# Gated slot attention kernel: queries held one place later than in time, and a new order at the end of each slot

## The chip, the cores and the metric

The kernel runs on one core of a Trainium2 chip. The metric is the device time of one execution in microseconds (us), and the kernel's time is the median of several executions. TensorE is called PE, its weight loads PEld, VectorE DVE, ScalarE ACT, GpSimd POOL, and SyncE, which issues most of the DMAs, SP.

## The reference

An attention layer with a gated two-state recurrence (B=4 sequences, T=512, 256 channels, H=16 heads of 128), a layer norm, a gated feed-forward layer with int8 weights, and a second layer norm. All is fp32. The core of it:

```python
def step(carry, xs):                       # per head, over time
    Sk, Sv = carry
    q_t, k_t, v_t, w_t, g_t, b_t = xs
    gt = jnp.exp(g_t)
    bw = b_t[:, :, None] * w_t
    Sk = Sk * gt[:, :, None, :] + k_t[..., :, None] * bw[:, :, None, :]
    Sv = Sv * gt[..., None] + bw[..., None] * v_t[:, :, None, :]
    s = jnp.einsum('bhd,bhdm->bhm', q_t, Sk) * SCALE
    a = jax.nn.softmax(s, axis=-1)
    o_t = jnp.einsum('bhm,bhmd->bhd', a, Sv)
    return ((Sk, Sv), o_t)
...
q = short_conv(h @ Wq, cq); k = short_conv(h @ Wk, ck)      # 4 taps, then silu
v = short_conv(h @ Wv, cv); w = short_conv(h @ Ww, cv)
g = jax.nn.log_sigmoid(h @ Wf1 @ Wf2)
beta = jax.nn.sigmoid(h @ Wb)
w = l2norm(rs(w, M))
...
o = gsa2_scan(q, k, v, w, g, beta)
o = o * rsqrt(mean(o * o) + EPS) * norm_w * sigmoid(h @ Wg1 @ Wg2 + bg2)
return o @ Wo
...
x = layernorm(x + attn(x));  x = layernorm(x + ffn(x))
```

## The kernel before, in words

A unit is one head of one sequence, so there are 64. The program runs in 68 slots. In each slot four units are in flight at different stages: `u1` (projections, convolutions, gates), `u2` (keys against queries, first scan), `u3` (softmax, second scan, output), `u4` (norm, gate, output projection), and `u5`, whose result is added to a sum in DRAM. Every engine has its own program, written out by hand: the order of the calls in the slot's loop over `r` (0 to 8) is the order on the engine, and engines meet by semaphores only. Buffers are few, and PSUM is fully used: `proj_ps` (2 banks), `tr_ps`, `V_ps`, `mix_ps` (2), `work_ps` (2).

A recurrence with decay is done without a loop over time, by blocks that double: 9 levels, of which levels 0 to 6 lie inside chunks of 128 places. At a level the queries of one block see the keys of the block before it. `U` holds the keys' weights as seen from the end of their block; they are grown on DVE level by level: `copy_U` copies the blocks that this level needs, `scale_U` multiplies the even blocks by the gates' products, in two instructions. For `u1` the levels 0 to 3 are grown at the end of a slot, for the same unit as `u2` levels 4 to 7 at the start of the next one.

The first scan (`level_scores` on PE, `descend` on DVE) goes from the largest block down and leaves the scores in `V_ps`: ACT copies them to `V`, PE turns them (`turn(1, V)`), DVE takes the rows' largest (`largest`, tile `mx`), ACT takes the exponentials (`exp_scores`, tile `aN`), PE turns `aN`, ACT copies that to `W`. The second scan goes up: `mix_products` on PE (W against U), `mix` on DVE (into `A2`, by masks), `grow_W` on POOL. `outputs` on PE adds the products of `A2` with the values and of `W` with the chunk states `Sv`.

A query at place t sees the keys up to and with t. In blocks this means that a block's queries are those from its predecessor's last place to its own last but one: the views are shifted by L - 1 places (`after_odd`). The last place of each chunk falls out of the second scan's views, so it has four products of one column (`mix_ends`), a copy of four columns (`mixable`, lev 0) and a growth of its own (`grow_W_ends`).

At the end of a slot ACT's order is: `oN` (copy of the attention output), `V`, then `tanh(act, u1, 2)`, which is the tanh of k and an instruction that adds 1; POOL multiplies k's two parts by that (`silu_qk`, i = 2, tile `qk`), and PE's `key_query` of the next slot waits for it. Every fourth slot a new head follows (`next_h`): there POOL also splits weights into two parts (`low_weights`, L370, and `low_f`, L387), and DVE takes `largest` of `u2` in the slot itself rather than at the start of the next.

At the end of the attention the feed-forward layer runs in 32 steps, and SP stores one sequence after another to `out`.

## Time and profile before

| | |
|---|---|
| median of 3 runs | 2008.67 us (2008.37 to 2124.88) |
| profiled execution | 2009.03 us |
| its span | 2007.3 us |
| PE busy | 1927.6 us (96%) |
| DVE busy | 1775.8 us (88%) |
| ACT busy | 1396.5 us (70%) |
| POOL busy | 1334.0 us (66%) |
| granted TensorE clock, mean | 0.984 |

Busy time is the sum of the times in which an engine has an instruction in it; instructions of one engine overlap by some tens of ns at their ends. The span is that of the profiled execution, from first to last instruction; 1.7 us of the execution lie outside it.

### The profile page before, as it was taken

The numbers are of one execution on the slowest core, as the hardware profiler recorded it, in microseconds if no ns is written. First come the engines' busy times: TensorE is split into PE (matmuls) and PEld (weight loads), VectorE is DVE, ScalarE is ACT, GpSimd is POOL, SyncE is SP. The second block draws the span as 40 slices with busy tenths as digits, with TensorE's granted clock in tenths as the row PEclk, the third lists the DMA queues.
The fourth block names the chain that finished last, engine by engine and source line by source line (L and its number), as shares of the span: only waits on it lengthen the run. The fifth ranks groups of instructions, "written<-read, shape, count | busy, mean of one in ns | idle before, by whom it ended". The sixth has DMA issues, their size and how long they took to land.

```text
span 2007.3 us, 41500 instructions
## 1 busy us (share of the span) xinstructions
PE 1927.6 (96%) x12192; PEld 1627.1 (81%) x12192; DVE 1775.8 (88%) x4096; ACT 1396.5 (70%) x3986; POOL 1334.0 (66%) x2289
## 2 busy tenths in 40 slices
PE   7899999999999999999999999999999999999697
PEld 5688888888888888888888888888888888887586
DVE  5599999999999999999999999999999999998487
ACT  4477777777777777777777777777777777776442
POOL 5367676767677676777677776777676766766343
PEclk8899999999999999999999999999999999999798
DMA  3011110111111111111111111111110111102300
GB/s 78 1 55 26 25 35 14 36 24 33 26 24 26 26 34 23 27 24 32 26 27 23 27 34 24 26 24 33 26 34 15 29 32 23 22 15 51 63 11 32
DMA packets 53645, 58.51 MB, mean 29 GB/s; under 512 B 14896, under 2 KB 44720, under 8 KB 53424
## 3 DMA queue, kind: packets, MB, share of 16 engines
q0 software_dynamic: 9216, 33.56, 11.4%
q1 hardware_dynamic: 44208, 22.29, 4.0%
q8 instruction: 104, 1.70, 0.4%
q14 instruction: 117, 0.96, 0.2%
HBM read 20.19 MB, written 37.75 MB: 29 GB/s over the span
## 4 chain that ended last, share of the span: by engine, by line
PE 82%; POOL 8%; DVE 5%; issue 3%; ACT 1%; DMA 1%; POOLq 0%; DVEq 0%; ACTq 0%
PE proj_ps L718 15%; PE mix_ps L802 11%; PE V_ps L773 10%; PE work_ps L927 8%; PE work_ps L933 7%; PE tr_ps L742 6%; PE V_ps L751 5%; PE work_ps L1569 5%; PE proj_ps L397 4%; PE work_ps L822 3%; PE mix_ps L809 2%; POOL w_lo L370 2%; PE tr_ps L782 2%; PE work_ps L824 2%; POOL qk L618 1%
## 5 line engine op out<-in xcount | busy, mean ns | idle before, releaser
L587 DVE SCALAR_TENSOR_TENSOR conv<-proj_ps,coefs,conv 128x511 f32<-128x511 f32 (+2 forms) x768 | 561.9, 732 | 9.5 <-ACT conv L347 2.6
L298 POOL TENSOR_TENSOR W<-W,tot 128x256 f32<-128x256 f32 x384 | 256.0, 667 | 244.0 <-PE mix_ps L802 243.9
L1053 POOL TENSOR_TENSOR A_lev<-A,masks 128x256 f32<-128x256 f32 x448 | 319.5, 718 | 0.1
L802 PE MATMUL mix_ps<-W,U 128*128 128x128 f32 x1792 | 295.3, 287 | 13.7 <-POOL W L298 8.2
L802 PEld LDWEIGHTS mix_ps<-W,U 128*128 128x128 f32 x1792 | 256.5, 192 | 40.2 <-issue 24.5
L773 PE MATMUL V_ps<-A_lev,UT 128*128 128x128 f32 x1792 | 285.9, 282 | 1.6 <-DVE V_ps L683 1.6
L711 DVE COPY_PREDICATED A<-masks,mix_ps 128x256 f32<-128x256 uint32 x448 | 268.7, 600 | 12.3 <-PE mix_ps L802 12.2
L580 DVE TENSOR_TENSOR wT<-wT,tot 128x128 f32<-128x128 f32 x768 | 233.3, 344 | 40.3 <-DVE U L563 1.8
L773 PEld LDWEIGHTS V_ps<-A_lev,UT 128*128 128x128 f32 x1792 | 237.4, 192 | 23.4 <-DVE V_ps L683 23.2
L356 ACT ACTIVATE th<-conv 128x512 f32<-128x512 f32 x256 | 162.3, 634 | 104.2 <-DVE conv L587 103.0
L718 PE MATMUL proj_ps<-hT_hi,w_hi 128*128 128x512 f32 x512 | 222.9, 435 | 4.5 <-DVE conv L587 2.7
L563 DVE COPY U<-wT 128x256 f32<-128x256 f32 x448 | 206.4, 461 | 7.2
L429 ACT ACTIVATE UT<-tr_ps 128x512 f32<-128x512 f32 (+1 forms) x256 | 139.1, 543 | 103.2 <-PE tr_ps L742 102.4
L683 DVE TENSOR_TENSOR V_ps<-V_ps,tot 128x256 f32<-128x256 f32 x384 | 164.1, 427 | 50.3 <-PE V_ps L773 50.0
L718 PE MATMUL proj_ps<-hT_hi,w_lo 128*128 128x512 f32 x512 | 203.2, 397 | 0.0
L718 PE MATMUL proj_ps<-hT_lo,w_hi 128*128 128x512 f32 x512 | 202.1, 395 | 0.0
L927 PE MATMUL work_ps<-qk 128*128 128x512 f32 (+3 forms) x512 | 182.1, 457 | 3.9 <-POOL qk L618 2.9
L298 POOL TENSOR_TENSOR W<-W,gT 128x256 f32<-128x256 f32 x64 | 54.3, 849 | 197.4 <-PE mix_ps L802 197.4
L347 ACT ACTIVATE conv<-proj_ps,coefs 128x512 f32<-128x512 f32 x256 | 175.6, 686 | 9.2 <-PE proj_ps L718 9.2
L414 ACT ACTIVATE A<-work_ps,fac 128x512 f32<-128x512 f32 (+3 forms) x256 | 128.2, 530 | 63.4 <-PE work_ps L927 63.1
L656 ACT ACTIVATE y_sb<-work_ps,rms 128x256 f32<-128x256 f32 x256 | 107.4, 472 | 63.0 <-PE work_ps L1569 58.8
L742 PE MATMUL tr_ps<-ident,U 128*128 128x128 f32 x896 | 140.1, 273 | 0.0
(200 smaller groups left out, 4774.0 us busy)
## 6 DMA issues: line engine op xcount, KB each, us to landing
head_sum<-y_sb POOLq DMA_DIRECT2D x64, 512.0 KB, 6.5
w_raw<-in_L_attn_Ww SPq DMA_DIRECT2D x16, 128.0 KB, 2.2
w_raw<-in_L_attn_Wq SPq DMA_DIRECT2D x16, 128.0 KB, 2.2
w_raw<-in_L_attn_Wk SPq DMA_DIRECT2D x16, 128.0 KB, 2.3
w_raw<-in_L_attn_Wv SPq DMA_DIRECT2D x16, 128.0 KB, 2.2
wo_raw<-in_L_attn_Wo SPq DMA_DIRECT2D x16, 128.0 KB, 2.0
head_sum<-in_L_attn_hidden_states SPq DMA_DIRECT2D x1, 2048.0 KB, 10.3
acc<-head_sum SPq DMA_DIRECT2D x4, 512.0 KB, 3.9
```

Source lines behind the costliest of these rows:

```text
L298: nc.gpsimd.tensor_tensor(w, w, block_tot(u3.par, lev, 0), ALU.mult).then_inc(W_step, 1)
L347: nc.scalar.activation(conv[:, CONV_BUF[i], :], proj_ps[:, CONV_BANK[i], :], ACT.Copy, scale=filt(u, i, KW - 1)).then_inc(tap_done, 1)
L563: nc.vector.tensor_copy(Ulev(u, lev).rearrange("p (n e l) -> p n e l", e=2, l=L), merged(X, lev))\
L580: nc.vector.tensor_tensor(x_, x_, odd_tot(u.par, lev, e), ALU.mult).then_inc(U_step, 1)
L587: nc.vector.scalar_tensor_tensor(y_, proj_ps[:, CONV_BANK[i], 0:T - back], filt(u, i, KW - 1 - back), y_, ALU.mult, ALU.add).then_inc(conv ...
L711: nc.vector.copy_predicated(dst, mask_cols(lev).bitcast(U32), mix_cols(lev % 2, lev)).then_inc(mix_done, 1)
L718: last = nc.tensor.matmul(dst, w[:, k, :], x_(k), start=(k == 0 and n == 0), stop=(k == KT - 1 and n == 2))
L742: last = nc.tensor.transpose(tr_ps[:, n * P:(n + 1) * P], block_, ident[:, :])
L773: last = nc.tensor.matmul(dst, UT[:, i % 2, at:at + P], A_lev[:, lev, 2 * p:2 * p + 2, :], start=False, stop=True, skip_group_check=True)
L802: last = nc.tensor.matmul(mix_ps[:, half, p * P:(p + 1) * P], Ulev(u3, lev)[:, p * P:(p + 1) * P], after_odd(W[:, p * T // 2:(p + 1) * T / ...
L927: nc.tensor.matmul(work_ps[:, A_BANK[c], c * P:T], qk[:, 1, c * P:(c + 1) * P], qk[:, 0, c * P:T], start=True, stop=True).then_inc(A_ps_re ...
L1053: nc.gpsimd.tensor_tensor(dst, diag_after_odd(lev), mask_cols(lev), ALU.mult)\
```

## The change

Queries are held one place later than in time: place t holds the query of time t - 1, and place 0 that of time T - 1. The first scan is as it was; the shift is made where `V_ps` is copied to `V`. In the second scan the blocks' queries are then simply the odd blocks (`odd` in place of `after_odd`), and no chunk's last place falls out: `mix_ends`, its copy on DVE and `grow_W_ends` on POOL are gone. The query of time T - 1 sees all keys, so there is a fourth chunk state (one more product in `chunk_states`, one more instruction in `states`) and one more product in `outputs`. The gate, the running sum in DRAM and the stores to `out` are shifted in the same way. `vT` has no buffer of its own any more.

Apart from this, ACT's order at a slot's end is changed, and DVE's `copy_U` of level 4 goes from the start of a slot to the end of the one before.

```diff
-            w = after_odd(W[:, :], lev)
+            w = odd(W[:, :], lev)
...
-        def grow_W_ends(pool, u3):
-
-            pool.wait_ge(ends_ready, u3.count(1, 1))
-            ends = W[:, :].rearrange("p (c t) -> p c t", t=P)[:, :, P - 1]
-            nc.gpsimd.tensor_tensor(ends, ends, tot[:, u3.par, T - 8:T - 4], ALU.mult).then_inc(W_step, 1)
...
             dve.wait_ge(tanh_done, u.count(4, 4))
             wait(dve, vT_ps_ready, u.count(1, 0))
+            wait(dve, aT_ps_ready, u.count(1, 0))
...
-            if lev == 0:
-                dve.wait_ge(ends_ready, u3.count(1, 1))
-                nc.vector.tensor_copy(A2[:, :, P - 1], mix_ps[:, 0, T // 2:T // 2 + C]).then_inc(far_done, 1)
...
-            dst = after_odd(A2[:, :, :].rearrange("p c t -> p (c t)"), lev).rearrange("p (c n) l -> p c n l", c=C)
+            dst = odd(A2[:, :, :].rearrange("p c t -> p (c t)"), lev).rearrange("p (c n) l -> p c n l", c=C)
...
-            for c, at in ((0, 2), (1, 1), (2, 3)):
+            for c, at in ((0, 2), (1, 1), (2, 3), (3, 4)):
                 last = nc.tensor.matmul(tr_ps[:, c * P:(c + 1) * P], UT_top[:, at, :], vN[:, u2.par % 2, c * P:(c + 1) * P],
                                         start=True, stop=True)
...
-        def mix_ends(pe, u3):
-
-            for c in range(C):
-                last = nc.tensor.matmul(mix_ps[:, 0, T // 2 + c:T // 2 + c + 1], chunk_of(U_chunks(u3), c),
-                                        W[:, (c + 1) * P - 1:(c + 1) * P], start=True, stop=True)
-            last.then_inc(ends_ready, 1)
...
                 if t:
                     last = nc.tensor.matmul(dst, W[:, cols], Sv[:, u3.par % 2, t - 1, :], start=False, stop=True)
+                else:
+                    last = nc.tensor.matmul(dst[0:1, :], W[:, 0:1], Sv[:, u3.par % 2, C - 1, :], start=False, stop=True,
+                                            skip_group_check=True)
...
-                nc.sync.dma_start(out_v[:, b * C:(b + 1) * C, :], acc[:, b * C:(b + 1) * C, :]).then_inc(ffn["store"], 16)
-            sp.wait_ge(ffn["store"], 16 * B)
+                nc.sync.dma_start(out[b, P - 1:T - 1, :].rearrange("(c p) n -> p c n", p=P), acc[:, b * C + 1:(b + 1) * C, :])\
+                    .then_inc(ffn["store"], 16)
+                nc.sync.dma_start(out[b, 0:P - 1, :], acc[1:P, b * C, :]).then_inc(ffn["store"], 16)
+                nc.sync.dma_start(out[b, T - 1:T, :], acc[0:1, b * C, :]).then_inc(ffn["store"], 16)
+            sp.wait_ge(ffn["store"], 16 * 3 * B)
...
                 for lev in range(GROWN_EARLY, LEVELS - 1):
-                    if u2:
+                    if u2 and lev == GROWN_EARLY:
+                        scale_U(dve, u2, lev)
+                    elif u2:
                         grow_U(dve, u2, lev)
```

The running sum's start value, one DMA of 2048 KB before, is now copied by six DMAs, one of them of 508 rows. The two low and high parts of the gate's input are made in three instructions instead of two, four times in all.

On DVE, around the end of a slot in which no new head follows; `Sv` are the chunk states, the `U` copies and the pairs of `wT` behind them the levels 2, 3 and so on, `mx` is `largest`. Before:

```order
L587 SCALAR_TENSOR_TENSOR conv<-proj_ps,coefs,conv 128x509
L695 SCALAR_TENSOR_TENSOR Sv<-Sv,tot,tr_ps 128x128 x2
L563 COPY U<-wT 128x256
L580 TENSOR_TENSOR wT<-wT,tot 128x32x4 x2
L563 COPY U<-wT 128x256
L580 TENSOR_TENSOR wT<-wT,tot 128x16x8 x2
L540 TENSOR_REDUCE mx<-work_ps 128x4
L563 COPY U<-wT 128x256
L580 TENSOR_TENSOR wT<-wT,tot 128x8x16 x2
```

Now:

```order
L585 SCALAR_TENSOR_TENSOR conv<-proj_ps,coefs,conv 128x509
L694 SCALAR_TENSOR_TENSOR Sv<-Sv,tot,tr_ps 128x128 x3
L561 COPY U<-wT 128x256
L578 TENSOR_TENSOR wT<-wT,tot 128x32x4 x2
L561 COPY U<-wT 128x256
L578 TENSOR_TENSOR wT<-wT,tot 128x16x8 x2
L561 COPY U<-wT 128x256
L538 TENSOR_REDUCE mx<-work_ps 128x4
L578 TENSOR_TENSOR wT<-wT,tot 128x8x16 x2
```

There is a third state, and the copy of level 4 now stands ahead of `mx`.

On ACT at the same place; `oN` is the attention output, `V` the scores, `th` k's tanh and then that plus 1, `tg` the gate of `u4`, `aN` the exponentials. Before:

```order
L1253 ACTIVATE Sv<-tr_ps 128x128
L1257 ACTIVATE oN<-work_ps 128x512
L1262 ACTIVATE V<-V_ps 128x512
L356 ACTIVATE th<-conv 128x512
L360 ACTIVATE th<-th 128x512
L1134 ACTIVATE tg<-proj_ps,bg_sb 128x512
```

Now:

```order
L1254 ACTIVATE Sv<-tr_ps 128x128
L354 ACTIVATE th<-conv 128x512
L358 ACTIVATE th<-th 128x512
L1261 ACTIVATE V<-V_ps 128x511
L1262 ACTIVATE V<-V_ps 128x1
L1266 ACTIVATE oN<-work_ps 128x512
L1135 ACTIVATE tg<-proj_ps,bg_sb 128x512
```

The two instructions on k went ahead of `V`, `V` became two instructions, and `oN` went behind it.

## Rows read from the trace of the kernel before

**Rows 1.** The page, the chain that ended last, share of each engine.

```profile
PE 82%; POOL 8%; DVE 5%; issue 3%; ACT 1%; DMA 1%; POOLq 0%; DVEq 0%; ACTq 0%
```

**Rows 2.** Chain in order of time, one slot: start us, us, what.

```profile
1012.83 0.68 PE work_ps L822 x4
1013.52 0.22 PE work_ps L824 x2
...
1015.81 0.66 PE work_ps L933 x4
1016.47 2.85 PE proj_ps L718 x12
1019.31 0.44 PE work_ps L933 x4
...
1022.72 0.79 PE mix_ps L809 x8
...
1047.94 1.56 PE work_ps L927 x4
```

**Rows 3.** Timeline of DVE: start us, us, engine, line, op [idle before it].

```profile
1013.52 0.78 DVE L695 SCALAR_TENSOR_TENSOR Sv<-Sv,tot,tr_ps 128x128 f32<-128x128 f32 x2
...
1015.54 0.49 DVE L580 TENSOR_TENSOR wT<-wT,tot 128x128 f32<-128x128 f32 x2
1016.50 0.69 DVE L540 TENSOR_REDUCE mx<-work_ps 128x4 f32<-128x512 f32 x1 [0.47 <-PE work_ps L933]
1017.11 0.79 DVE L563 COPY U<-wT 128x256 f32<-128x256 f32 x1
1018.01 0.84 DVE L580 TENSOR_TENSOR wT<-wT,tot 128x128 f32<-128x128 f32 x2
1018.89 0.29 DVE L563 COPY U<-wT 128x256 f32<-128x256 f32 x1
...
1025.53 0.36 DVE L677 TENSOR_SCALAR V_ps<-V_ps,tot 128x129 f32<-128x129 f32 x1
```

**Rows 4.** Timeline of POOL in the same stretch.

```profile
1014.52 1.37 POOL L637 TENSOR_TENSOR tot<-tot 128x32 f32<-128x32 f32 x4
1017.01 1.49 POOL L618 TENSOR_TENSOR qk<-th,conv 128x256 f32<-128x256 f32 x2 [1.12 <-ACT th L360]
```

**Rows 5.** Timeline of ACT in the same stretch.

```profile
1015.16 0.59 ACT L1262 ACTIVATE V<-V_ps 128x512 f32<-128x512 f32 x1
1015.64 0.63 ACT L356 ACTIVATE th<-conv 128x512 f32<-128x512 f32 x1
...
1017.41 0.36 ACT L404 ACTIVATE aN<-work_ps,mx 128x128 f32<-128x128 f32 x1
...
1018.69 0.22 ACT L404 ACTIVATION_READ_ACCUMULATOR aN<-work_ps,mx 128x1 f32 x1
```

**Rows 6.** Timelines of DVE and POOL where a new head follows.

```profile
1042.63 1.10 DVE L580 TENSOR_TENSOR wT<-wT,tot 128x128 f32<-128x128 f32 x2
...
1044.53 0.69 DVE L540 TENSOR_REDUCE mx<-work_ps 128x4 f32<-128x512 f32 x1
...
1043.55 1.52 POOL L370 TENSOR_TENSOR w_lo<-w_raw,w_hi 128x256 fp32r<-128x256 f32 x2
...
1046.37 1.52 POOL L618 TENSOR_TENSOR qk<-th,conv 128x256 f32<-128x256 f32 x2
```

**Rows 7.** Groups of instructions: count, busy us, mean ns, idle before.

```profile
L809 PE MATMUL mix_ps<-W,wT 128*128 128x1 f32 x512 | 61.6, 241 | 0.0
L706 DVE COPY A<-mix_ps 128x4 f32<-128x4 f32 x64 | 9.9, 155 | 6.3 <-PE mix_ps L809 6.3
L1241 ACT ACTIVATE bg_sb<-bg_sb 128x16 f32<-128x16 f32 x1 | 0.2, 226 | 0.0
```

**Rows 8.** Waits: who for whom, us in total, times, longest.

```profile
POOL qk L618 <- ACT th L360: 63.0, 49, 6.5
```

**Rows 9.** The page's DMA issues: count, KB each, us to landing.

```profile
out_x<-acc SPq DMA_DIRECT2D x4, 512.0 KB, 3.1
```

More of the change, by code:

```diff
@@ L214, in pairs, with odd @@
             return ap.rearrange("p (n e l) -> p n e l", e=2, l=1 << lev)
+        def odd(ap, lev):
+            return pairs(ap, lev)[:, :, 1, :]
         def after_odd(ap, lev):
@@ L593, in silu_w @@
             dve.wait_ge(tanh_done, u.count(4, 1))
-            wait(dve, ends_ready, u.count(1, 1 - 2))
+            wait(dve, UT_ps_ready, u.count(6, 2 - 12))
             wait(dve, mix_ps_ready, u.count(7, 1 - 14))
@@ L622, in gates @@
             act.wait_ge(fexp_done, u1.count(1, 1))
-            wait(act, W_step, u1.count(8, 1 - 16))
+            wait(act, W_step, u1.count(7, 1 - 14))
             wait(act, V_step, u1.count(10, -10))
@@ L630, in gate_products @@
                 pool.wait_ge(gate_set, u1.count(1, 1))
-                wait(pool, Sv_step, u1.count(2, 2 - 8))
+                wait(pool, Sv_step, u1.count(3, 3 - 12))
             else:
@@ L670, in descend @@
             if r == 0:
-                wait(dve, V_done, u2.count(1, 0))
+                wait(dve, V_done, u2.count(2, 0))
                 nc.vector.memset(V_ps[:, 0:P], 0.0).then_inc(V_step, 1)
@@ L733, in turn_U @@
             if i == 0:
-                wait(pe, Sv_step, u2.count(2, 0))
+                wait(pe, Sv_step, u2.count(3, 0))
                 pe.wait_ge(U_step, u2.count(22, 22))
@@ L869, in first_copies @@
         def first_copies(act, b):
-            for i, dst in enumerate((f1_hi, g1_hi)):
-                act.wait_ge(first_ps, 2 * b + i + 1)
-                nc.scalar.activation(dst[:, b * T:(b + 1) * T], mix_ps[:, i, :], ACT.Copy).then_inc(first_sb, 1)
-        def first_lows(dve, b):
-            cols = slice(b * T, (b + 1) * T)
-            for i, (dst, high_) in enumerate(((f1_lo, f1_hi), (g1_lo, g1_hi))):
-                dve.wait_ge(first_sb, 2 * b + i + 1)
-                nc.vector.tensor_tensor(dst[:, cols], mix_ps[:, i, :], high_[:, cols].bitcast(F32), ALU.subtract)\
-                    .then_inc(first_lo, 1)
+            act.wait_ge(first_ps, 2 * b + 1)
+            nc.scalar.activation(f1_hi[:, b * T:(b + 1) * T], mix_ps[:, 0, :], ACT.Copy).then_inc(first_sb, 1)
+            act.wait_ge(first_ps, 2 * b + 2)
+            nc.scalar.activation(g1_hi[:, b * T + 1:(b + 1) * T], mix_ps[:, 1, 0:T - 1], ACT.Copy).then_inc(first_sb, 1)
+            nc.scalar.activation(g1_hi[:, b * T:b * T + 1], mix_ps[:, 1, T - 1:T], ACT.Copy).then_inc(first_sb, 1)
+        def first_lows(dve, b):
+            whole, moved, last_ = slice(b * T, (b + 1) * T), slice(b * T + 1, (b + 1) * T), slice(b * T, b * T + 1)
+            dve.wait_ge(first_sb, 3 * b + 1)
+            nc.vector.tensor_tensor(f1_lo[:, whole], mix_ps[:, 0, :], f1_hi[:, whole].bitcast(F32), ALU.subtract)\
+                .then_inc(first_lo, 1)
+            dve.wait_ge(first_sb, 3 * b + 3)
+            nc.vector.tensor_tensor(g1_lo[:, moved], mix_ps[:, 1, 0:T - 1], g1_hi[:, moved].bitcast(F32), ALU.subtract)\
+                .then_inc(first_lo, 1)
+            nc.vector.tensor_tensor(g1_lo[:, last_], mix_ps[:, 1, T - 1:T], g1_hi[:, last_].bitcast(F32), ALU.subtract)\
+                .then_inc(first_lo, 1)
         def beta_products(pe, b):
-            pe.wait_ge(first_lo, 2 * b + 1)
+            pe.wait_ge(first_lo, 3 * b + 1)
             high, low = setup_weights(setup_hi_sb), setup_weights(setup_lo_sb)
@@ L988, in _ @@
                 if h == 1:
-                    nc.sync.dma_start(head_sum[:, :, :], x_v).then_inc(sum_set, 16)
+                    rows = head_sum.rearrange("p (b c) n -> p b c n", c=C)
+                    nc.sync.dma_start(rows[1:P, :, 0, :], x[:, 0:P - 1, :].rearrange("b p n -> p b n")).then_inc(sum_set, 16)
+                    nc.sync.dma_start(rows[0:1, :, 0, :], x[:, T - 1:T, :].rearrange("b p n -> p b n")).then_inc(sum_set, 16)
+                    for b in range(B):
+                        nc.sync.dma_start(rows[:, b, 1:C, :], x[b, P - 1:T - 1, :].rearrange("(c p) n -> p c n", p=P))\
+                            .then_inc(sum_set, 16)
                 nc.sync.dma_start(wg_raw[:, :], Wg2[:, bass.ts(h, P)]).then_inc(head_g, 16)
@@ L1253, in _ @@
                         nc.scalar.activation(Sv[:, u2.par % 2, 0, :], tr_ps[:, 0:P], ACT.Copy).then_inc(KV_done, 1)
+                if u1:
+                    tanh(act, u1, 2)
+                if u2:
+                    act.wait_ge(V_ps_ready, u2.count(9, 9))
+                    wait(act, s_ps_ready, u2.count(1, 0))
+                    nc.scalar.activation(V[:, 1:T], V_ps[:, 0:T - 1], ACT.Copy).then_inc(V_done, 1)
+                    nc.scalar.activation(V[:, 0:1], V_ps[:, T - 1:T], ACT.Copy).then_inc(V_done, 1)
                 if u3:
@@ L1257, in _ @@
                     nc.scalar.activation(oN[:, :], work_ps[:, 0, :], ACT.Copy).then_inc(oN_done, 1)
-                if u2:
-                    act.wait_ge(V_ps_ready, u2.count(9, 9))
-                    wait(act, s_ps_ready, u2.count(1, 0))
-                    nc.scalar.activation(V[:, :], V_ps[:, :], ACT.Copy).then_inc(V_done, 1)
-                if u1:
-                    tanh(act, u1, 2)
             act.wait_ge(ffn["scales"], 2)
@@ L1498, in _ @@
                 if u3:
-                    mix_ends(pe, u3)
                     mix_products(pe, u3, 1)
@@ L1591, in _ @@
                 if u2:
[L1593 removed]
+                    pe.wait_ge(V_done, u2.count(2, 2))
                     if u4:
```

45 lines of the change are left out of this document (20 added, 25 removed).

## The prediction

> **What bounds the kernel now.** The first view is the chain that ended last: 82% of it lies on TensorE (PE) and 8% on POOL [rows 1]. That says "PE", but not which of PE's instructions could go without another engine taking the end over, so the second view is the chain in order of time through one slot [rows 2], and the third the timelines of the other engines beside it. A slot takes about 28 us: `mx` starts at 1016.50 [rows 3] and at 1044.53 one slot later [rows 6]. PE has no gap over 0.1 us in it, but some of its groups take longer than their products do, since their weights were loaded only after a wait: the turn of V takes 0.66 us for four products (at 1015.81) [rows 2] where the turn of `aN` takes 0.44 (at 1019.31) [rows 2].
>
> Two loops leave PE at a slot's end and come back. The reader should see how tight both are. First: V is copied by ACT until 1015.75 [rows 5], PE turns it until 1016.47, `mx` starts at 1016.50, ACT's exponentials run from 1017.41 to 18.91 [rows 5], and PE, busy with projections until 1019.31 [rows 2], then turns `aN`. So this path has only 0.4 us to spare, for which PE's own projections of 2.85 us are the cover. Second: behind `mx` DVE works through U's growth and the convolutions without a wait until `V_ps` at 1025.53 [rows 3], the step that PE waits for at the scan's second product. What DVE does there ends when PE comes, give or take 0.2 us.
>
> A third thing to see is that some DVE instructions stretch while POOL works. The copy at 1017.11 takes 0.79 us, the same at 1018.89 takes 0.29, the pair at 1018.01 takes 0.84, the pair at 1015.54 0.49 [rows 3]; POOL's `qk` runs from 1017.01 to 1018.50 [rows 4], over just the slow ones. Together `qk` costs DVE 0.85 us.
>
> **Part by part, in a slot without a new head behind it.** The sum is made from the last step of the second scan, before which nothing moves.
>
> PE, removed: `mix_ends`, 0.79 us of the chain (at 1022.72) [rows 2], 61.6 us of busy time in all [rows 7]. Behind it stands the product of level 1, which needs POOL's first growth; that is ready about when `mix_ends` starts now, so I take 0.72 us as gained, with 0.5 and 0.79 as bounds.
>
> PE, added: one product in `chunk_states` and one in `outputs`, each 0.22 us (L824 x2 (at 1013.52) [rows 2]; the second has one weight column, and its price lies between 0 and this; I take 0.22, as its moving side is as long). The one in `chunk_states` is hidden: the group at 1012.83 takes 0.68 us where two of the pairs of 0.22 would take 0.44, since it waits for DVE's last mix. So +0.22.
>
> ACT: V's copy becomes two instructions. The second writes one column; the nearest row is an ACT instruction of 16 columns, 0.23 us [rows 7], of which about half overlaps the one ahead. V's copy at 1015.16 now follows on `oN`'s; it will follow on PE's product, which comes 0.22 later. Turn of V: +0.27 us in all (between 0.2 and 0.45), from 1016.47 to 1016.74. There is no cover: PE waits for V now and will. That k's tanh goes first costs nothing on ACT, whose two instructions of about 0.63 us each (at 1015.64) [rows 5] fit before PE's product; `oN` behind V isn't read before the next slot.
>
> POOL, removed: the growth of the ends, estimated at 0.15 us, as DVE's instruction on as few columns [rows 7]. Moved: `qk`. It waits for k's tanh for 63.0 us in 49 slots now [rows 8]; with that ready well over 1 us earlier, it will start as soon as POOL's gate products end (1014.52 + 1.37 - 0.15 = 1015.74 [rows 4]) and run to about 1017.2.
>
> DVE, removed: a copy of 0.155 us, 0.06 of it not overlapped [rows 7]. Added: one state, 0.4 us (half of 0.78 (at 1013.52) [rows 3]), which nothing covers but the 0.47 us that DVE waits ahead of `mx` [rows 3]. Moved into the same 0.47 us: level 4's copy, 0.29 + 0.1 us. And `qk` now falls on the pair of level 3 and that copy, which cost 0.85 us more there and as much less behind `mx`. So `mx` starts at 1016.03 (end of the pair at 1015.54) + 0.4 + 0.39 + 0.85 = 1017.7, where it could start at 1016.8: the wait that the copy should fill is filled nearly three times over.
>
> What that gives. `mx` takes 0.69, the exponentials 1.5, so `aN` is ready at 1019.9, and its turn, with a late load of weights as V's has, ends 0.72 us later, at 1020.6. It ends at 1019.75 now: +0.87. Less 0.72 for `mix_ends`, PE comes to the scan's second product 0.15 to 0.2 us later than now, not earlier. DVE, which has its copy of level 4 and the collision behind it, is where it was (-0.1). **So +0.2 us in such a slot**, of which there are two in four.
>
> **Where a new head follows**, `mx` stands before the pair of level 3, POOL is busy with weights until 1045.07, and DVE's pair and copy are slow ahead of `mx` already (1.10 us for the pair [rows 6]). There `mx` comes 0.6 later (the state, and 0.2 by other collisions), and the exponentials still make it, since PE's cover is 0.4 and V's turn is 0.27 later itself. POOL's `qk`, which holds PE up there now (it ends at 1047.89 [rows 6], and PE's group takes 1.56 at 1047.94 [rows 2]), ends 0.15 earlier and is waited for no more. But DVE's whole row is 0.7 us later by then, since `qk` strikes it wherever it is and no work was taken out. DVE comes to the scan's second product last: **+0.55 us**. In the slot behind it POOL has one more piece of weights, `qk` ends later and hits the same pair and copy: `mx` is 1.3 us later. I take **+0.4 us**.
>
> Four slots: 2 x 0.2 + 0.55 + 0.4 = 1.35 us, and 16 such: +22 us.
>
> **Ends.** The last store, 512 KB, lands 3.1 us after its issue [rows 9]. Now three stores follow one another, with two more issues, +0.9 us if the data flow as before. One of them has 127 rows of 1 KB, a number that can't be dealt out to 16 DMA engines evenly. From the row, 512 packets on 16 engines in under 3.1 us, thus 32 on each, are at most 0.1 us each, and more likely half that, as some of the 3.1 is latency; all 127 on one engine would be 5 to 6 us instead. Bounds +0.9 and +5.5; I take +3. The six copies for the running sum are issued once, behind the first head, and eight small instructions of setup at 0.16 to 0.23 us [rows 7] lie beside other work: nothing, and if that cover is gone, 1 to 2 us once.
>
> On this the Trainium skill has a rule against the change ("DMA: Bandwidth & Descriptors", "Why a DMA increments its semaphore by 16 and not by 1"): an SP transfer is spread over the largest number of engines up to 16 that divides the slowest dimension, and 127 partitions go to one. No DMA in the profile has such a shape, so the trace neither agrees nor disagrees; by that rule the end costs the upper bound, and the sum is 2.5 us more.
>
> Sum: 2009.0 (profiled execution) + 22 + 3 = 2034. The profiled execution is 0.4 us over the median of 2008.67, so I say **2034 us** against that median, +1.3%. A measurement of this kernel tells about 2% (40 us) from no change. The likeliest case's own range is 2018 to 2048.
>
> **Rivals.**
> - PE's sum decides (chance 0.25). If `mx` isn't late, each slot gains 0.72 - 0.27 = 0.45 us: 64 x 0.45 = 29 us, with the end 1983. For it speaks the 82% on PE, and that DVE's 0.47 us of waiting is just there; against it, that it needs DVE's copy and pair to stay quick although `qk` falls on them, which they do not in rows 3 and 4. If `qk` were as late as now, this would be the case.
> - The two cancel (0.15). The state and the copy make `mx` late, but by no more than the cover of 0.4 and 0.27 us in the common slots: 2000 to 2015.
> - DVE falls behind everywhere (0.10). DVE's quick copies and POOL hold each other up, so `qk` starts later than 1015.74. From a start of some 1016.1 on its second half covers the copy of level 4 too, and `mx` comes 0.5 us later again: 48 slots x 0.5 = 24 us more, 2058. For it: one more instruction on an engine that waits little; against: the gate products are four short instructions [rows 4].
> - The new views change the cost of the block operations (0.03). Aligned odd blocks may be read faster by POOL, DVE or PE than shifted ones. A gain of 0.1 us in each of DVE's seven mixes would give 64 x 0.7 = 45 us where DVE decides, 1960 to 1990. No row shows an aligned one.
>
> **How the numbers follow.** Forecast 0.47, the rivals as above. The range takes in the forecast's case, the cancelling one and most of the first rival, and leaves out some 0.1 on each side: 1984 to 2048. Faster by over 2% (under 1968) only in the last rival and the far end of the first: 0.03. Slower by over 2% (over 2049): the third rival and the edge of the forecast's own case, 0.12. Within 2%: 0.85.
>
> **What the changed profile would show.** (1) `mix_ends` gone and nothing waiting in its place, PE's product of level 1 right behind the turn of U. (2) `qk` on POOL without a wait for ACT, starting about 1.2 us earlier against the end of the second scan. (3) The pair of level 3 and the copy of level 4 stretched, those behind `mx` quick. (4) DVE's wait ahead of `mx` gone, and `mx` about 0.9 us after the turn of V; it starts 0.03 after it now. (5) A new wait of PE, of about 0.6 us in three slots of four, for the exponentials. (6) At the end, a store of 127 rows that lands 5 us or more after its issue. The prediction is wrong if (5) is missing, that is, if `mx` is late by less than 0.5 us; then the first rival's sum holds.

## The result, and the profile after

The changed kernel takes 2025.12 us in the median (2022.34 to 2025.4, 5 runs), the kernel before beside it 2010.38. One of the five executions of the kernel before took 2124.88 us, far from the other four, and does not count in the ratio. The ratio is 1.0072, with a 95% interval of 1.0058 to 1.0087: slower by some 14.5 us, which is real and less than 2%. The forecast was 2034, that is 25 us slower. The profiled execution's span grew from 2007.27 to 2020.61 us, by 13.3.

The first line is the page's chain of waits by engine. It answers to [rows 1].

```profile
PE 68%; POOL 11%; DVE 11%; issue 5%; ACT 2%; DMA 1%; POOLq 0%; DVEq 0%; ACTq 0%
```

TensorE's share fell from 82% to 68%; DVE (5 to 11%) and POOL (8 to 11%) took most of what it lost. So the ownership of the end moved, while the time hardly did. The chain in order of time (start us, us, what) through the slot that answers to [rows 2]:

```profile
1016.67 0.34 PE work_ps L809 x2
1017.01 0.31 PE work_ps L813 x2
1017.32 0.42 PE work_ps L809 x2
...
1020.05 0.66 PE work_ps L929 x4
1020.70 2.75 PE proj_ps L714 x12
1023.46 0.02 issue
1023.47 0.66 PE work_ps L929 x4
1024.13 1.39 PE work_ps L923 x4
...
1026.89 0.22 PE tr_ps L738 x2
1027.11 0.03 issue
1027.13 0.69 PE mix_ps L797 x4
...
1029.70 0.71 PE V_ps L747 x4
```

`mix_ends` is gone, and the product of level 1 (1027.13) stands right behind U's turn. The last line is the scan's second product. The same product in the kernel before:

```profile
1025.95 0.71 PE V_ps L751 x4
```

The new product with one column of weights is L813; the profile has two records for each of these products, hence its x2. The turn of `aN` (1023.47) now takes 0.66 us where it took 0.44 [rows 2]: its weights are loaded late, after the exponentials.

DVE, POOL and ACT in the same slot, by their timelines (start us, us, engine, line, operation, idle before), for [rows 3 to 5]:

```profile
1017.23 1.23 DVE L694 SCALAR_TENSOR_TENSOR Sv<-Sv,tot,tr_ps 128x128 f32<-128x128 f32 x3
...
1019.30 0.71 DVE L561 COPY U<-wT 128x256 f32<-128x256 f32 x1
1020.11 0.84 DVE L578 TENSOR_TENSOR wT<-wT,tot 128x128 f32<-128x128 f32 x2
1020.99 0.29 DVE L561 COPY U<-wT 128x256 f32<-128x256 f32 x1
1021.20 0.68 DVE L538 TENSOR_REDUCE mx<-work_ps 128x4 f32<-128x512 f32 x1
...
1017.98 1.14 POOL L636 TENSOR_TENSOR tot<-tot 128x32 f32<-128x32 f32 x4
1019.08 1.52 POOL L617 TENSOR_TENSOR qk<-th,conv 128x256 f32<-128x256 f32 x2
...
1019.33 0.60 ACT L1261 ACTIVATE V<-V_ps 128x511 f32<-128x511 f32 x1 [0.70 <-PE V_ps L769]
1019.83 0.16 ACT L1262 ACTIVATE V<-V_ps 128x1 f32<-128x1 f32 x1
...
1021.91 0.37 ACT L402 ACTIVATE aN<-work_ps,mx 128x128 f32<-128x128 f32 x1 [0.85 <-DVE mx L538]
```

`qk` runs from 1019.08, without a wait for ACT. The copy of level 3 and the pair behind it, which overlap it, are the stretched instructions; the next copy takes 0.29. `mx` has no idle time ahead of it and starts 0.50 us after V's turn (1020.70). The waits (who for whom, us in total, times, longest) say who pays:

```profile
PEld work_ps L929 <- ACT aN L402: 29.7, 48, 1.6
PE work_ps L929 <- ACT aN L402: 14.1, 21, 4.8
DVE V_ps L676 <- PE V_ps L747: 21.8, 47, 1.8
```

The first is new in 48 of 64 slots, three of each four. Of its 0.62 us a slot TensorE loses only 0.24 in a common slot, nearly all of it the late load in the chain (0.66 for 0.44). In the slot behind a new head it also waits for 0.38 us, so it loses 0.60 there. The third says that DVE now waits in the scan, by 0.46 us in the same slots: behind `mx` it is no longer the late one.

**Slots by kind.** In every fourth slot a new head follows; the slot behind it is the next one, and the other two of four are called common. I took from each trace the medians over five slots of each kind, in us from the end of the last `mix` of the slot before; "2nd product" is the start of the first weight load of the scan's second product. The last column is the slot's length for four slots in a row, added.

| kernel | `mx`, common | `mx`, new head follows | `mx`, slot behind it | 2nd product, common | ..., new head follows | ..., behind it | four slots |
|---|---|---|---|---|---|---|---|
| before | 3.88 | 3.88 | 3.88 | 13.31 | 13.63 | 13.29 | 112.22 |
| after | 4.86 | 4.40 | 5.22 | 13.36 | 14.03 | 13.73 | 112.50 |

Up to the second product the four slots lose 0.05 + 0.05 + 0.40 + 0.44 = 0.94 us. From there to the next last `mix` each gives back 0.16 us (14.70 to 14.54 in a common slot), 0.64 in all. Net, 0.3 us in four slots, 16 times: some 5 us. The trace has it as 6.4 us between the first and the last copy of V (1765.34 to 1771.77).

**The end.** The timeline of SP's queue shows the last stores, where [rows 9] had one of 512 KB:

```profile
2010.76 0.39 SPq L1011 DMA_DIRECT2D out_x<-acc  x1
2011.19 0.33 SPq L1013 DMA_DIRECT2D out_x<-acc  x1
2011.57 3.19 SPq L1014 DMA_DIRECT2D out_x<-acc  x1
```

The span ends at 2020.61, 9.85 us after the first of these was issued; before it ended 3.17 us after its issue (2004.10 to 2007.27). The last norm takes the same 1.38 us in both, so the end costs 6.7 us. What the DMA engines moved between 2010 and 2021, in 40 equal pieces of that window, is the second line here:

```profile
DMA  0000008999100000000000000000000000000000
GB/s 0 0 0 0 0 0 302 380 380 343 22 4 0 4 4 4 22 26 22 26 22 26 22 26 22 26 22 26 22 26 22 26 22 26 22 7 0 0 0 0
```

384 KB go in 1.1 us at up to 380 GB/s, where the 512 KB of before went at up to 389; then, after a pause of some 1.5 us, 127 KB take 5.3 us at 22 to 26 GB/s, a sixteenth (each piece is 0.275 us). That is the rate of one of the 16 engines, so the 127 rows went through one. That is what the Trainium skill's rule says of such a shape ("DMA: Bandwidth & Descriptors", "Why a DMA increments its semaphore by 16 and not by 1"), and the trace now agrees.

So the 13.3 us of the span are 6.4 in the slots, 6.7 at the end, 1.2 ahead of the first slot (V's first copy starts at 89.3 and not 88.1; over all kernels here it lies anywhere from 86.1 to 92.7, so this one is no effect) and -1.0 in the feed-forward part.

### The profile page after: what moved, and what is told of

Read it like the earlier page. It is cut to its first block, busy times and chain, and to the rows that moved or that the text cites. A ratio compares the mean times of both kernels' runs of the same rounds, so it can differ in the third digit from the quotient of the medians.

```text
span 2020.6 us, 41004 instructions
## 1 busy us (share of the span) xinstructions
PE 1927.2 (95%) x11936; PEld 1585.7 (78%) x11936; DVE 1749.2 (87%) x4100; ACT 1397.3 (69%) x4054; POOL 1321.8 (65%) x2225
## 4 chain that ended last, share of the span: by engine, by line
PE 68%; POOL 11%; DVE 11%; issue 5%; ACT 2%; DMA 1%; POOLq 0%; DVEq 0%; ACTq 0%
PE proj_ps L714 13%; PE mix_ps L797 11%; PE V_ps L769 8%; PE work_ps L929 7%; PE work_ps L923 6%; PE tr_ps L738 6%; PE V_ps L747 5%; PE work_ps L1574 4%; PE proj_ps L395 3%; DVE wT L578 2%; DVE conv L585 2%; POOL w_lo L368 2%; POOL qk L613 2%; PE work_ps L809 2%; POOL fac L1083 2%
## 5 line engine op out<-in xcount | busy, mean ns | idle before, releaser
L302 POOL TENSOR_TENSOR W<-W,tot 128x256 f32<-128x256 f32 x384 | 251.8, 656 | 191.0 <-PE mix_ps L797 179.7
L797 PE MATMUL mix_ps<-W,U 128*128 128x128 f32 x1792 | 287.3, 283 | 14.8 <-POOL W L302 8.9
L578 DVE TENSOR_TENSOR wT<-wT,tot 128x128 f32<-128x128 f32 x768 | 240.0, 353 | 35.1 <-DVE U L561 1.4
L707 DVE COPY_PREDICATED A<-masks,mix_ps 128x256 f32<-128x256 uint32 x448 | 231.6, 517 | 18.8 <-PE mix_ps L797 18.8
L561 DVE COPY U<-wT 128x256 f32<-128x256 f32 x448 | 188.4, 421 | 8.9
```

Of the source, the lines that this page charges most:

```text
L302: nc.gpsimd.tensor_tensor(w, w, block_tot(u3.par, lev, 0), ALU.mult).then_inc(W_step, 1)
L561: nc.vector.tensor_copy(Ulev(u, lev).rearrange("p (n e l) -> p n e l", e=2, l=L), merged(X, lev))\
L578: nc.vector.tensor_tensor(x_, x_, odd_tot(u.par, lev, e), ALU.mult).then_inc(U_step, 1)
L707: nc.vector.copy_predicated(dst, mask_cols(lev).bitcast(U32), mix_cols(lev % 2, lev)).then_inc(mix_done, 1)
L797: last = nc.tensor.matmul(mix_ps[:, half, p * P:(p + 1) * P], Ulev(u3, lev)[:, p * P:(p + 1) * P], odd(W[:, p * T // 2:(p + 1) * T // 2], ...
```

## The experiments

All ratios are against runs of the kernel before on the same chip.

### One or both of the reorderings undone, on the changed kernel

**act_back** puts ScalarE's old order back:

```diff
-                if u1:
-                    tanh(act, u1, 2)
+                if u3:
...
+                    nc.scalar.activation(oN[:, :], work_ps[:, 0, :], ACT.Copy).then_inc(oN_done, 1)
...
-                if u3:
...
-                    nc.scalar.activation(oN[:, :], work_ps[:, 0, :], ACT.Copy).then_inc(oN_done, 1)
+                if u1:
+                    tanh(act, u1, 2)
```

> ScalarE's order of before (oN, V, then k's tanh) on the changed kernel. Theory A (GpSimd's product for k's part of qk, started early by the early tanh, holds up VectorE's copy and pair ahead of mx, so that TensorE waits for the exponentials): TensorE's wait for the exponentials falls from 44 us to under 15, the pair of level 3 and the copy of level 4 are quick again, and the time falls by 8 to 18 us, to 2007 to 2017. Theory B (the longer way to V, one more product in the output and a second V copy, costs the time, whatever the order): V's turn is no earlier, rather 0.1 us later since oN stands ahead of it again, and the time stays within 3 us of 2025.

**copy_back** puts level 4's copy back at the start of the next slot:

```diff
-                    if u2 and lev == GROWN_EARLY:
-                        scale_U(dve, u2, lev)
-                    elif u2:
+                    if u2:
                         grow_U(dve, u2, lev)
...
                         scale_U(dve, u1, 3)
-                        copy_U(dve, u1, 4)
```

> The copy of level 4 of U back at the start of the slot, behind mx, on the changed kernel; all else as changed. Theory A: mx starts 0.3 us earlier in three slots of four, the wait for the exponentials falls by 0.3 x 48 = 14 us, and the time by 5 to 14 us, to 2011 to 2020. Theory B: no change within 3 us.

**shift_alone** does both, so that of the change only the shift is left.

> Both orders of before on the changed kernel, so that only the shift of the queries is left. Theory A: no wait for the exponentials to speak of, TensorE gains 0.7 us by the four removed products and pays 0.5 on the way to V: 2000 to 2010 with the longer end still in it. Theory B: 2022 or more, the shift itself is the loss.

Measured: act_back 2025.9 us, ratio 1.0070 [1.0058, 1.0082]; copy_back 2016.67, 1.0019 [1.0011, 1.0028]; shift_alone 2035.98, 1.0119 [1.0106, 1.0133]. The copy's old place is worth 8.5 us on the changed kernel, as theory A expected. The other two came out at the times of their theories B, but not for B's reason in act_back: ScalarE's old order changes nothing in the time where the copy is ahead of `mx`, and costs 19 us where it isn't. The shift alone is the slowest of the four.

The waits of act_back tell why it isn't quicker:

```profile
PEld V_ps L747 <- DVE V_ps L676: 31.0, 63, 0.6
PE V_ps L747 <- DVE V_ps L676: 16.0, 59, 0.4
PE work_ps L929 <- ACT aN L402: 5.4, 2, 4.8
```

TensorE's wait for the exponentials is as rare as in the kernel before (3 times, 5.9 us), as theory A had it. `mx` comes at 4.44 to 4.48. But `qk` then strikes DVE behind `mx`, and TensorE waits for DVE at the scan's second product in 59 slots, where the changed kernel has that wait in 15. One wait took the other's place.

Waits of shift_alone:

```profile
PEld V_ps L747 <- DVE V_ps L676: 37.0, 62, 0.6
PE V_ps L747 <- DVE V_ps L676: 22.2, 60, 0.4
```

TensorE itself waits for DVE at the scan's second product in 60 slots, a wait that the kernel before has twice. `mx` is in time there (4.44 to 4.60), and the second product comes at 13.63 to 14.08. With ScalarE's new order (copy_back) it comes at 13.15 in common slots: `qk` strikes DVE ahead of `mx`, partly in DVE's idle time, and not in the row behind it. That is what the new order gives. My prediction took the collision off the row behind `mx` too, but gave that no worth.

### The reorderings alone, on the kernel before

**before_act** makes ScalarE's new order in the kernel before (the diff of act_back turned round), **before_copy** moves level 4's copy there (the diff of copy_back turned round).

> The kernel before, with ScalarE's new order alone (tanh of k, copy of V, then the attention output's copy); no shift, level 4's copy at its old place. Theory A (qk's collision with DVE is cheaper ahead of mx, where DVE has 0.47 us of waiting, than behind it, where DVE's row meets PE at the second product): faster than before by 0.1 to 0.35 us a slot, 1988 to 2004 against 2012 in these runs; mx starts 0.3 to 0.5 us later after the last mix than now. Theory B (PE's own sum fixes the slot in the kernel before, with or without the collision): within 2007 to 2016. Theory C (the late mx makes PE wait for the exponentials by more than it gives back): 2018 to 2035.

> The kernel before, with the copy of level 4 of the growth moved ahead of mx alone; ScalarE's old order, no shift. qk then still falls behind mx, and the copy is a quick one (about 0.3 us). Theory A (DVE's row behind mx is what decides at the second product, as the run with both old orders said): the row behind mx gets 0.3 to 0.4 us shorter, mx no later than PE's cover of 0.4 us allows, 1990 to 2006 against 2012. Theory B (PE's sum decides): within 2007 to 2016. Theory C (mx is late past the cover): 2018 to 2030.

Measured: before_act 2012.46 us, 1.0007 [0.9998, 1.0015]; before_copy 2011.67, 1.0002 [0.9993, 1.0011]. Both are nothing, theory B. The wait of DVE in the scan, first in before_act, then in before_copy, shows where the work saved on DVE went:

```profile
DVE V_ps L677 <- PE V_ps L751: 25.5, 48, 1.1
```

```profile
DVE V_ps L677 <- PE V_ps L751: 11.3, 46, 1.1
```

DVE comes 0.5 and 0.25 us early and waits for TensorE. In the kernel before TensorE's own work fixes a common slot, and DVE is just not late.

### What the step of the last columns was worth

**ends_out** takes `mix_ends`, the ends' growth and the far copy out of the kernel before, with the waits for them, and puts nothing in, so the last place of each chunk lacks that part of its scores. **ends_out_moved** has the two reorderings as well.

```diff
                 if u3:
-                    grow_W_ends(pool, u3)
...
                 if u3:
-                    mix_ends(pe, u3)
                     mix_products(pe, u3, 1)
...
-                dve.wait_ge(ends_ready, u3.count(1, 1))
-                nc.vector.tensor_copy(A2[:, :, P - 1], mix_ps[:, 0, T // 2:T // 2 + C]).then_inc(far_done, 1)
```

> The kernel before with the step of the chunks' last columns left out: mix_ends on TensorE, the ends' growth on POOL, the far copy on DVE, and their waits; no shift takes its place, so the last column of each chunk lacks that part of its scores. In the kernel before DVE waits for the scan's first product by next to nothing and TensorE for DVE by next to nothing. Theory A (the two are balanced there, so a TensorE that comes 0.7 us earlier finds DVE's row not ready): most of the 0.7 us is lost in a new wait of TensorE for DVE (V_ps, chunk 2's scaling), the slot gains at most 0.3 us: 1993 to 2010 against 2011. Theory B (TensorE alone decides): 64 x 0.7 = 45 us faster, 1960 to 1972.

> The same as ends_out (the step of the last columns left out), with ScalarE's new order and the moved copy of level 4 on top, neither of which moved the time of the kernel before by itself. Theory A (each of the two makes DVE's row behind mx shorter, by 0.5 and 0.25 us in their own traces, which is worth something only when TensorE comes early): 0.3 to 0.6 us a slot faster than ends_out, 1968 to 1985. Theory B (TensorE's wait for the exponentials takes what DVE gives): within 8 us of ends_out.

Measured: ends_out 2005.97 us, 0.9977 [0.9966, 0.9989], theory A; ends_out_moved 2018.5, 1.0033 [1.0021, 1.0044], which neither theory had. A step that held TensorE for 0.79 us a slot [rows 2] and 50 us in all is worth 5 us when it goes.

In one of the two common slots of ends_out, and behind a new head, the second product comes at 13.06, only 0.25 earlier, and in the other common slot at 13.1 to 13.2. Its waits say why:

```profile
PEld V_ps L748 <- DVE V_ps L677: 37.2, 62, 0.6
PE V_ps L748 <- DVE V_ps L677: 22.3, 60, 0.4
```

And where a new head follows it comes at 14.00, 0.37 later than before, though work was only taken away. The timelines of DVE and POOL in such a slot of ends_out, whose last `mix` ended at 1038.02:

```profile
1039.61 0.75 DVE L563 COPY U<-wT 128x256 f32<-128x256 f32 x1
...
1043.37 0.87 DVE L563 COPY U<-wT 128x256 f32<-128x256 f32 x1
...
1039.48 0.73 POOL L370 TENSOR_TENSOR w_lo<-w_raw,w_hi 128x256 fp32r<-128x256 f32 x1
...
1043.35 1.48 POOL L618 TENSOR_TENSOR qk<-th,conv 128x256 f32<-128x256 f32 x2
```

and in the kernel before, where it ended at 1040.65:

```profile
1042.24 0.29 DVE L563 COPY U<-wT 128x256 f32<-128x256 f32 x1
...
1045.66 0.29 DVE L563 COPY U<-wT 128x256 f32<-128x256 f32 x1
...
1042.27 0.85 POOL L370 TENSOR_TENSOR w_lo<-w_raw,w_hi 128x256 fp32r<-128x256 f32 x1
```

Before, DVE's copy at 1042.24 was 0.03 us ahead of POOL's instruction and ran in 0.29, and POOL's took 0.85. Without the ends' growth POOL is some 0.15 us earlier, gets there first, and the same copy takes 0.75; `qk`, 0.38 earlier, strikes the copy behind `mx`, which takes 0.87. Two collisions of 0.46 and 0.58 come with taking 0.15 us off POOL. What they cost in the end is the 0.37: this is read from the order of the rows, and no run moved POOL's instruction alone.

With the reorderings on top DVE is early again in common slots, but now `mx` is late, up to 5.19 in the slot behind a new head, and TensorE waits for the exponentials (ends_out_moved):

```profile
PEld work_ps L928 <- ACT aN L404: 46.4, 62, 1.4
PE work_ps L928 <- ACT aN L404: 26.0, 46, 4.6
```

So the two reorderings, harmless in the kernel before, cost 12.5 us on ends_out. They were made where TensorE comes early, and there its other loop, over `mx`, has no slack. Which of the two costs it there was not run.

### One more state on DVE

**before_state** adds to the kernel before an instruction of a state's form whose result nothing reads:

```diff
+        spare = sb("spare", [P, P])
...
                         states(dve, u2, 0)
+                        dve.wait_ge(Sv_step, u2.count(2, 1))
+                        nc.vector.scalar_tensor_tensor(spare[:, :], Sv[:, u2.par % 2, 1, :], chunk_tot(u2.par, 2),
+                                                       tr_ps[:, 2 * P:3 * P], ALU.mult, ALU.add)
                         states(dve, u2, 1)
```

> The kernel before with one more instruction of DVE a slot, between its two states: the same form as a state (128x128, about 0.4 us), written to a spare tile that nothing reads. Nothing else. Theory A (DVE's row is as long as TensorE's at the scan's first products, so what is added to DVE counts, although DVE is not on the chain): 0.2 to 0.4 us a slot, 2024 to 2037 against 2011. Theory B (the 0.47 us that DVE waits ahead of mx takes it in): 2008 to 2016.

Measured: 2021.06 us, 1.0044 [1.0031, 1.0056], between the two theories. The slots by kind settle it: the second product is at 13.29 in the common slots and behind a new head, as before, and at 14.21 where a new head follows, 0.58 later. 16 x 0.58 = 9.3 us is the whole effect (9.9 measured). The state is free where DVE idles ahead of `mx`, three slots of four. In the fourth it costs more than its own 0.4.

### The alignment of the blocks

The shift makes the blocks of each level start on a multiple of their length. The groups of DVE's mixes (count, busy us, mean ns, idle before), of the changed kernel and then of the kernel before:

```profile
L707 DVE COPY_PREDICATED A<-masks,mix_ps 128x256 f32<-128x256 uint32 x448 | 231.6, 517 | 18.8 <-PE mix_ps L797 18.8
```

```profile
L711 DVE COPY_PREDICATED A<-masks,mix_ps 128x256 f32<-128x256 uint32 x448 | 268.7, 600 | 12.3 <-PE mix_ps L802 12.2
```

**mix_unaligned** writes them to the old places, so that its scores are off by a column:

```diff
-            dst = odd(A2[:, :, :].rearrange("p c t -> p (c t)"), lev).rearrange("p (c n) l -> p c n l", c=C)
+            dst = after_odd(A2[:, :, :].rearrange("p c t -> p (c t)"), lev).rearrange("p (c n) l -> p c n l", c=C)
```

> The changed kernel, with DVE's mixes written to the odd blocks of the old alignment (one place later) again; everything else as in the changed kernel. What this changes in the computation: the mixes land one column off, so the output isn't the reference's; the number, shapes and waits of all instructions stay. In the changed kernel the mixes of levels 2 to 4 take about 0.43 us each where they took 0.73, 0.59 and 0.52 before. Theory A (the alignment of the block is what made them quick, and it is worth time because DVE's last mixes stand on the way to the last product of the second scan): these three go back to 0.73, 0.59 and 0.52 us, and the slot gets 0.15 to 0.6 us longer, which over 64 slots gives 2035 to 2062 against about 2026. Theory B (the mixes are quick but PE's products hide them): durations go back, the time stays within 2020 to 2030. Theory C (the durations come from something else, such as less POOL work beside them): durations stay at about 0.43.

Measured: 2027.72 us, 1.0087 [1.0074, 1.0100]; the interval overlaps that of the changed kernel, 1.0058 to 1.0087. Its mixes:

```profile
L707 DVE COPY_PREDICATED A<-masks,mix_ps 128x256 f32<-128x256 uint32 x448 | 269.3, 601 | 18.4 <-PE mix_ps L797 18.3
```

Theory B: the place written to does make the mixes quicker, 37 us of DVE's busy time, and it is worth some 1.5 us by the slots of the profiled executions and 3 us by the ratios, neither clear of the noise. The 0.16 us a slot that the shift gives back has another source, as mix_unaligned keeps nearly all of it (14.57 from the second product to the last `mix`, before 14.70). It isn't that the ends' step is gone, as ends_out still takes 14.71; nor the two reorderings, as shift_alone takes 14.55. What is left is the shift itself, and TensorE and POOL read `W` in the same blocks. The chain at the product of level 2, behind the scan's second one, of the kernel before and then of the changed one:

```profile
1026.66 0.54 PE mix_ps L802 x4
```

```profile
1030.41 0.45 PE mix_ps L797 x4
```

These products of 128 columns follow one another at 134 ns before and at 111 ns after, a median over all slots; at level 3 at 117 and 112, and at the other five levels the pitch is the same within 1 ns. At level 2 that is 0.09 us. Most of the rest, some 0.05, comes one level later: the product takes 0.45 us instead of 0.47, and the idle time ahead of the next one is 0.05 instead of 0.08, behind POOL's growth of `W`, which takes 644 ns instead of 665. 64 x 0.16 = 10 us, which hides as much of the change's price. That it is the alignment of the blocks that are read is argued from these rows: no run put TensorE's and POOL's reads back to the old places.

### The store

**store_split** deals the 127 rows out as 112 and 15:

```diff
-                nc.sync.dma_start(out[b, 0:P - 1, :], acc[1:P, b * C, :]).then_inc(ffn["store"], 16)
+                nc.sync.dma_start(out[b, 0:112, :], acc[1:113, b * C, :]).then_inc(ffn["store"], 16)
+                nc.sync.dma_start(out[b, 112:P - 1, :], acc[113:P, b * C, :]).then_inc(ffn["store"], 16)
...
-            sp.wait_ge(ffn["store"], 16 * 3 * B)
+            sp.wait_ge(ffn["store"], 16 * 4 * B)
```

> The store of 127 rows as two, of 112 and of 15 rows, on the changed kernel. Theory A (127 rows go through one DMA engine): from the last norm to the end 10.3 us become 4.5 to 6, and the time falls by 4.5 to 6 us, to 2019 to 2021. Theory C (the end is long since three stores follow one another, the last of one row): it grows by another issue of 0.4 us.

Measured: 2016.95 us, 1.0034 [1.0021, 1.0047], 8 us less than the changed kernel and a little under theory A's 2019 to 2021. Its first store is issued at 2011.68 and its span ends at 2015.14, 3.5 us later, although four issues follow one another:

```profile
2011.68 0.39 SPq L1011 DMA_DIRECT2D out_x<-acc  x1
2012.12 0.48 SPq L1013 DMA_DIRECT2D out_x<-acc  x1
2012.65 0.46 SPq L1014 DMA_DIRECT2D out_x<-acc  x1
2013.15 0.26 SPq L1015 DMA_DIRECT2D out_x<-acc  x1
```

The end itself is thus 6.4 us shorter (9.85 to 3.46); the other 1.6 are within the noise of the two ratios.

### Both repairs, and a turn in another order

**copyback_store** is the changed kernel with copy_back's and store_split's edits. **turn_last** is that, with V's chunks turned so that the one-column copy is waited for last:

```diff
-                    pe.wait_ge(V_done, u2.count(2, 2))
+                    pe.wait_ge(V_done, u2.count(2, 1))
...
-                    turn(1, V).then_inc(s_ps_ready, 1)
+                    for c in (1, 2, 3, 0):
+                        if c == 0:
+                            pe.wait_ge(V_done, u2.count(2, 2))
+                        last = nc.tensor.transpose(work_ps[:, 1, c * P:(c + 1) * P], V[:, c * P:(c + 1) * P], ident[:, :])
+                    last.then_inc(s_ps_ready, 1)
```

> The changed kernel with level 4's copy back at its old place and the store of 127 rows split into 112 and 15. The two edits apart gave -8.5 and -8 us. Theory A (they act in different places, one in each slot and one at the end): they add, 2006 to 2012, and so as quick as the kernel before or up to 0.3% quicker. Theory B (part of either is a change of the whole schedule and not of its place): 2013 to 2019.

> The changed kernel with level 4's copy at its old place and the 127-row store split (2007.2 as it stands), and TensorE turns V's chunks in the order 1, 2, 3, 0, so that only the last of the four turns waits for ScalarE's one-column copy. Theory A (the copy of one column, 0.16 us, is on TensorE's way at V's turn in each slot): 0.1 to 0.16 us a slot, 1997 to 2002. Theory B (DVE's row behind mx decides, V's turn is covered): 2004 to 2010.

Measured: copyback_store 2007.24 us, 0.9983 [0.9974, 0.9991]; the two repairs add, and the shift is then as quick as the kernel before or a little quicker. turn_last 2005.94, 0.9969 [0.9958, 0.9981]: the quickest kernel here that computes the whole, 0.3% below the kernel before. Between these two the intervals overlap. The turn is worth 1.3 us by the two medians and 3 us by the ratios, which is not clear of the noise and less than theory A asked for; the time lies where theory B had it.

## Why the prediction was right, and where it was not

The direction and the range held, and the time was 9 us too high. That it still fell into the forecast's own case owes something to luck: the slots lost 6.4 us of the 22 forecast, the end 6.7 where I took 3, and the one error made up for part of the other. Its steps, one by one:

- **"`mix_ends` gone and nothing waiting in its place" (1)**: so in the chain. In the changed kernel the way from the turn of `aN` to the scan's second product got 0.63 us shorter (1019.75 to 1025.95, now 1024.13 to 1029.70), near the 0.72 that I took. But they are no gain that could be counted on alone. ends_out shows them in the kernel before: 0.25 in a common slot, and 0.37 lost where a new head follows, since DVE is right behind.
- **V's turn, +0.27, bounds 0.2 to 0.45**: it ends 4.36 after the last `mix`, before 3.84, so +0.52, out of the bounds. V's copy starts 0.45 later (2.99, before 2.54) and the one-column copy adds 0.07. The product with one column of weights is no cheap one, nor is the product behind it (0.31 and 0.42 in the chain, where a product of `outputs` takes 0.22): `outputs`, from its first product to the scan's next, takes 2.18 us (1016.67 to 1018.85), before 1.80 (0.68 and five of 0.22 [rows 2]), so +0.38 where I took +0.22.
- **`qk` early, on the pair of level 3 and a copy ahead of `mx` (2, 3)**: right, but for which copy. It starts 2.74 after the last `mix`, before 4.39, so 1.65 earlier and not 1.2; so it strikes the copy of level 3 and the pair, and leaves level 4's copy at 0.29.
- **`mx` late (4) and a new wait for the exponentials in three slots of four (5)**: right in place and count (48 times). TensorE itself loses 0.24 us by it in a common slot and 0.60 behind a new head, where I had 0.6 throughout. `mx` is 0.50 after V's turn and not 0.9, since the turn itself is later. `mx` alone went from 3.88 to 4.86, by 0.98; I had 1.2 (1017.7 against 1016.50 [rows 3]). The 1.64 us put ahead of `mx` fill the wait of 0.47 three and a half times over, not "nearly three times".
- **The sum for a slot up to the second product**: +0.2, +0.2, +0.55, +0.4 forecast; 0.05, 0.05, 0.40 and 0.44 measured. In a common slot TensorE's own path decides, as DVE waits there: the turn of `aN` ends 0.67 us later and not 0.87 (7.12 after the last `mix`, now 7.79), and 0.63 of that is won back. Where a new head follows, DVE comes last, as forecast: the wait of TensorE for DVE at the second product stands in 15 slots.
- **The rival "the new views change the cost of the block operations" (0.03)**: this is the step that failed. I took it as an alternative, and priced it on DVE's mixes alone. It holds beside the forecast, and through TensorE's products and POOL's growth: -0.16 us in each slot, -10 us. Forecast 22 us for the slots, with this 12, measured 6. The remaining 6 are the way up to the second product: 1.35 us in four slots forecast, 0.94 measured.
- **"Then the first rival's sum holds", if (5) is missing**: act_back and shift_alone answer that. The wait for the exponentials is missing in their slots, and they take 2025.9 and 2036 us, not 1983, since DVE's row behind `mx` is then the late one.
- **The end, +3, bounds 0.9 and 5.5 (6)**: 6.7, above both bounds. The rule that I named there against the change was right, and I had put it aside for a middle value. Without the single engine the split shows +0.3 (3.17 to 3.5 us), under my lower bound: the issues go on while the first store flows.
- **ScalarE's new order** was called free on ACT and harmful through `qk`. The runs show that it is worth 19 us under the shift with the copy at its old place (copy_back against shift_alone), and nothing with the copy ahead of `mx` (the changed kernel against act_back). The added state was to cost 0.4 in each slot unless covered; before_state shows it covered in three of four, and at 0.58 in the fourth.

So the 50 us of TensorE's time that `mix_ends` took were lost in two steps: DVE's row stands right behind (ends_out), and the shift pays for the rest in outputs, V's turn, a state and a store.

The slots of the profiled executions lose 6.4 us and my count by kinds 5, since medians leave out the odd slot: in three common slots of the changed kernel `mx` comes at 5.19 to 5.49 and the second product at 13.69 to 14.00, 1.6 us in all. Why it does so in these three is open, and so is how much of the -1.0 us in the feed-forward part belongs to the change. No run tests either.

## What to carry to other kernels

Before taking a step off the engine that the chain names, find the engine that is waited for next and read how long it idles, slot kind by slot kind: here 0.79 us off TensorE was worth 0.25 in one kind of slot and less than nothing in another. An edit that does nothing alone can be worth 1% beside another, in either direction, when two engines come to the same point within some tenths of a us, so test the parts on both kernels. When a layout moves by one row, look at the stores' leading dimension first: 127 rows in one DMA cost as much as the rest of the change.

## What the runs showed of the hardware

- A COPY of 128x256 on DVE takes 0.29 us alone and up to 0.87 where it starts with a POOL instruction under way; it then ends about 0.15 us after that one (1020.01 behind `qk`'s first half, which ends near 1019.85). In the trace of the kernel before 193 of the 195 stretched copies (over 0.33 us) among `U`'s 448 copies end so, 0.14 to 0.20 us behind POOL's instruction. Who starts first wins: a lead of 0.03 us gave DVE 0.29 and POOL 0.85; without it DVE took 0.75 and POOL 0.73. The Trainium skill says that the two share DVE's second port and block each other ("Advanced Engine Details and Errata", "VectorE Performance Modes"); the rows agree. That the outcome hangs on 0.1 us of phase I had not expected.
- A predicated copy into odd blocks takes 430, 426 and 443 ns at levels 2 to 4 when the blocks are aligned to their length, and 730, 586 and 518 ns when they lie one place off (medians); at levels 5 and 6 it takes 436 and 436 against 472 and 448, and at levels 0 and 1 the two agree within 1 ns. With the same change of blocks TensorE's products of 128 columns went from 134 to 111 ns at level 2 and from 117 to 112 at level 3.
- A product with one column of weights is not cheaper than a full one: L813 takes 0.31 us in the chain where a full product takes 0.22, and the product behind it 0.42, as its weights, unlike those of its neighbours, were loaded only after an idle time of 0.22 us of PEld.
- A store of 127 rows of 1 KB moves at 22 to 26 GB/s, one of 112 and one of 15 behind 384 KB at 250 to 390 (the piece in which they end at 238).
